# The first layer's experts moved from per-sequence masking to gathered slots, in a two-layer gated attention and expert kernel

## The reference

```python
x = x + tanh(g_xattn[0]) * cross(ctx, layernorm(x))      # u = 0: 16 heads, masked keys from ctx
x = x + tanh(g_ffn[0])   * ffn0(layernorm(x))            # u = 1
x = x + tanh(g_xattn[1]) * joint(layernorm(x), ctx)      # u = 2: keys of ctx and of x
x = x + tanh(g_ffn[1])   * ffn1(layernorm(x))            # u = 3: causal, then gated experts

def ffn0(x):                                             # the block that is changed
    attn_out = attention(x @ W_qkv + b_qkv)              # 16 heads of 16
    gate = softmax(x @ W_gate + b_gate)                  # 8 experts
    top_g, top_i = top_k(gate, 2)
    combine = sum(one_hot(top_i) * top_g)                # not normalised again
    expert_out = einsum('bsd,edf->bsef', x, W_experts) + b_experts
    return attn_out + einsum('bsef,bse->bsf', expert_out, combine)
```

## Time and profile before

| | us |
|---|---|
| median of 3 runs | 2615.38 |
| lowest and highest | 2613.62, 2620.35 |
| profiled execution, its own time | 2617.61 |
| its span, first to last instruction | 2615.9 |
| mean granted TensorE clock | 0.937 of full |
| PE busy in the span | 2282.1 (87%) |
| DVE busy | 1686.8 (64%) |
| ACT busy | 1362.3 (52%) |
| POOL busy | 978.5 (37%) |

### The profile page before, as it was taken

One profiled execution on the slowest core, in us unless ns is written; L12 is line 12 of the kernel. 1 busy time (PEld: TensorE's weight loads), 2 busy tenths in 40 slices (PEclk: granted clock), 3 DMA queues, 4 the chain that ended last, 5 costly groups with the idle time before them and its releaser, 6 DMA issues. The chain is left out here.

```text
span 2615.9 us, 52259 instructions
## 1 busy us (share of the span) xinstructions
PE 2282.1 (87%) x17492; PEld 1575.9 (60%) x17493; DVE 1686.8 (64%) x4481; ACT 1362.3 (52%) x2398; POOL 978.5 (37%) x1850
## 2 busy tenths in 40 slices
PE   2889999899999999999999999899848999999910
PEld 1445555555455556666666666666538999999910
DVE  4878886676767666777767668767563444443458
ACT  3889863454336346777777777767601222222211
POOL 5555412213122225333322247878602333333321
PEclk7999998999899999999999999999958999999965
DMA  7878623315134245544455445555180111111144
GB/s 216 206 192 208 148 67 82 88 38 122 30 88 95 65 99 135 116 116 113 112 118 120 107 116 109 122 133 129 42 277 27 34 36 37 36 36 32 35 173 156
DMA packets 209839, 275.49 MB, mean 105 GB/s; under 512 B 32606, under 2 KB 156489, under 8 KB 203370
## 3 DMA queue, kind: packets, MB, share of 16 engines
q1 hardware_dynamic: 196074, 242.38, 37.3%
q0 software_dynamic: 6912, 17.97, 2.2%
q10 hardware_dynamic: 6656, 12.58, 1.3%
HBM read 193.12 MB, written 80.64 MB: 105 GB/s over the span
## 5 line engine op out<-in xcount | busy, mean ns | idle before, releaser
L1035 ACT ACTIVATE ex<-t_ps 128x512 f32<-128x512 f32 (+1 forms) x1280 | 685.7, 579 | 203.0 <-PE t_ps L941 157.9
L1183 DVE TENSOR_REDUCE mx<-s_ps 128x2 f32<-128x512 f32 (+1 forms) x1024 | 659.9, 683 | 197.2 <-PE s_ps L912 125.2
L941 PE MATMUL t_ps<-qs,ks 123*128 123x256 bf16 x2048 | 355.5, 277 | 8.7 <-ACT ex L1035 3.7
L964 PE MATMUL pv_ps<-ex,va 128*17 128x256 f32 (+1 forms) x5120 | 318.1, 374 | 1.3 <-POOL ex L1087 1.3
L1029 ACT ACTIVATE qs<-tr_ps 27x2048 bf16<-27x2048 bf16 x128 | 239.2, 1869 | 108.3 <-PE tr_ps L925 105.5
L882 PE MATMUL pre_ps<-wexp,xt 128*128 128x512 f32 x512 | 270.5, 634 | 3.1 <-DVE moe L1242 2.2
L941 PEld LDWEIGHTS t_ps<-qs,ks 123*128 123x128 bf16 x2048 | 176.9, 98 | 156.1 <-ACT ex L1035 68.2
L1582 PEld LDWEIGHTS x_up_ps<-x_rows_t,x_wnow 128*128 128x128 f32 x2272 | 266.4, 193 | 5.3 <-issue 0.9
L1582 PE MATMUL x_up_ps<-x_rows_t,x_wnow 128*128 128x128 f32 x2272 | 267.0, 276 | 1.1 <-DVE x_pre L1645 0.7
L1592 PE MATMUL x_y_ps<-wdn,x_act 128*128 x1136 | 257.1, 379 | 0.7 <-DVE x_y L1653 0.7
L1612 ACT ACTIVATE x_rows_t<-x_rt_ps 128x256 f32<-128x256 f32 x72 | 27.6, 383 | 436.7 <-PE x_rt_ps L1571 436.7
(11 more groups left out here) (248 smaller groups left out, 3739.7 us busy)
## 6 DMA issues: line engine op xcount, KB each, us to landing
q_parts<-pq SPq DMA_DIRECT2D x128, 192.0 KB
qs<-q_parts SPq DMA_DIRECT2D x64, 384.0 KB, 4.9
qs<-q_parts SPq DMA_DIRECT2D x192, 128.0 KB, 5.8
k_parts<-pk SPq DMA_DIRECT2D x96, 192.0 KB
ks<-k_parts SPq DMA_DIRECT2D x96, 192.0 KB
ks<-k_parts SPq DMA_DIRECT2D x288, 64.0 KB
ks<-ctx_k_parts SPq DMA_DIRECT2D x64, 192.0 KB
ks<-ctx_k_parts SPq DMA_DIRECT2D x192, 64.0 KB
```

The lines of the kernel that those rows point to most:

```text
L941: last = pe.matmul(dst[:, t * T:(t + 1) * T], key[0:ROWS, h, t * P:(t + 1) * P], qs[q_at][0:ROWS, h, :], start=True, stop=True)
L964: last = pe.matmul(pv_ps[i * VS:i * VS + VW, q0:T], val[:, t, k * QH + i, :], e, start=r == 0 and t == 0, stop=r == srcs - 1 and t == NT - ...
L1035: act.activation(ex[:, n % EXPS, 0:w], t_ps[n % 2][:, 0:w], ACT.Exp).then_inc(t_read, 1)
L1183: dve.tensor_reduce(dst, s_ps[n % S_BANKS][:, :].rearrange("p (a b) -> p a b", a=dst.shape[-1]), AX.X, ALU.max).then_inc(s_read, 1)
```

## The change

The first layer's experts are run by slots as the second layer's are.

- **Cross jobs** (u = 0) get a tail after FIN: HNS, HNP and HNX normalise the updated x into `o`, STOREN writes it to memory, HT turns it (PE, ACT) and HG computes the gate logits of all tokens (PE, DVE).
- **Self jobs** no longer normalise x; LOADN brings the stored rows. GATE, GEXP, TOP, CT, MBIAS and EXPERT are gone, and FIN no longer adds the experts' share.
- **A chain for all tokens at once** begins when all sixteen HG are done: 23 RC steps on DVE with RX (ACT), RANK (PE), and sixteen RH, TH, NAME triples that find the row that each of 71 x 128 slots holds.
- **71 tiles** stand among self jobs 2 to 7 in the schedule's order (`tile_job`), 12 a job: XR gathers 128 rows (POOL, indirect DMA), XTT turns them (PE, ACT), XE multiplies by one expert's matrix, picked by a register loaded on PE and on DVE, and adds its bias (DVE), XS scatters the rows (POOL, indirect DMA).
- **Joint jobs** get LOADY and MOE: each token's two rows come back and are added to x with their weights by four DVE operations. LOADY of the first two jobs waits for all scatters.
- The second layer's `w1` and `wo` now share memory with the first layer's experts and are loaded at the first causal job's LOADX.

```diff
@@ STAGES, tile_job
+    "STOREN": [("sp", 0.5), ("wire", 6.0)], "LOADN": [("sp", 0.5), ("wire", 5.0)], "LOADY": [("sp", 0.5), ("wire", 6.5)], "MOE": [("dve", 1.95)],
+    "RC": [("dve", 0.95)], "RX": [("act", 0.42)], "RANK": [("pe", 0.9), ("dve", 0.72)],
+    "RH": [("dve", 0.67)], "TH": [("dve", 0.45), ("pool", 0.8)], "NAME": [("pe", 0.9), ("dve", 0.25)],
+    "XR": [("pool", 1.1), ("wire", 3.0)], "XTT": [("pe", 0.22), ("act", 0.39)], "XE": [("pe", 0.87), ("dve", 0.45)], "XS": [("pool", 1.1), ("wire", 3.5)],
+HOTS = 4
+CHUNKS = TOPK * TILES // HOTS
+NER, NY = 4, 3
+CHAIN = 23
+def tile_job(n):
+    return 1, 2 + n // 12
@@ job_steps
+    if u == 1:
+        s = add("LOADN", 0, ("STOREN", 0, b, 0), past("XT", 2))
+    else:
+        if u == 2:
+            y = add("LOADY", 0, *([("MOE", u, b - 2, 0)] if b >= 2 else [("XS", *tile_job(n), n) for n in range(SLOT_TILES)]))
+            x = add("MOE", 0, x, y)
...
-    if u == 1:
-        chain = add("GEXP", 0, add("GATE", 0, turned, ("FIN", u, b - 2, 0) if b >= 2 else None))
-        for n in range(TOPS):
-            chain = add("TOP", n, chain)
-        chain = add("MBIAS", 0, add("CT", 0, chain))
-        experts = [add("EXPERT", (t, e), chain) for t in range(NT) for e in range(0, E, 2)]
...
+    if u in (0, 3):
+        s = add("HNX", 0, add("HNP", 0, add("HNS", 0, s, ("HNX", u, b - 2, 0) if b >= 2 else None)))
+        if u == 0:
+            add("STOREN", 0, s)
+            s = add("HT", 0, s, past("HG", NQ))
@@ expert_steps
+    for n in range(SLOT_TILES):
+        add(of("XR", n), rc(CHAIN - 1), of("XTT", n - NER))
+        add(of("XTT", n), of("XR", n), of("XE", n - 2))
+        add(of("XE", n), of("XTT", n), of("XS", n - NY))
+        add(of("XS", n), of("XE", n))
@@ PE
-                    elif name == "EXPERT":
-                        t, e = k
-                        end_pre(step, pe.matmul(bank[:, :], xt_now[:, turn, t * P:(t + 1) * P], wexp[:, turn, e:e + 2, :].rearrange("p e n -> p (e n)"),
-                                                start=turn == 0, stop=ends), ends)
+                    elif name == "XTT":
+                        pe.wait_ge(er_loaded[k % NER], 16 * (k // NER + 1))
+                        for c in range(DC):
+                            last = pe.transpose(bank[:, c * P:(c + 1) * P], er[k % NER][:, c * P:(c + 1) * P], ident[:, :])
                         end_pre(step, last)
+                    elif name == "XE":
+                        wait_copied(pe, ("XTT", u, b, k))
+                        x = pe.value_load(expert_of[0:1, k:k + 1], min_val=0, max_val=E - 1)
+                        for c in range(DC):
+                            last = pe.matmul(bank[:, 0:D], ert[k % 2][:, c, :], wexp[:, c, bass.ds(x, 1), :].rearrange("p e n -> p (e n)"),
+                                             start=c == 0, stop=c == DC - 1)
+                        end_pre(step, last)
@@ POOL
+                    elif name == "XR":
+                        if k >= NER:
+                            wait_turned(pool, ("XTT", *tile_job(k - NER), k - NER))
+                        pool.indirect_dma_start(er[k % NER], None, n1_d.rearrange("b p t n -> (b p t) n"),
+                                                bass.IndirectOffsetOnAxis(ap=row_of[:, k:k + 1].bitcast(U32), axis=0)).then_inc(er_loaded[k % NER], 16)
+                    elif name == "XS":
+                        wait_copied(pool, ("XE", u, b, k))
+                        pool.indirect_dma_start(y1_d.rearrange("b p t n -> (b p t) n"), bass.IndirectOffsetOnAxis(ap=dest_of[:, k:k + 1], axis=0),
+                                                ey[k % NY], None, bounds_check=ROWS_OUT - 1, oob_is_err=False).then_inc(y_stored[k % NY], 16)
@@ DVE
+                    elif name == "XE":
+                        x = dve.value_load(expert_of[0:1, k:k + 1], min_val=0, max_val=E - 1)
+                        end_pre(step, dve.tensor_tensor(ey[k % NY], bank[:, 0:D], bexp[:, bass.ds(x, 1), :].rearrange("p e n -> p (e n)"), ALU.add))
+                    elif name == "MOE":
+                        for m in range(TOPK):
+                            for t in range(NT):
+                                last = dve.scalar_tensor_tensor(out=xs[x_at][:, t, :], in0=yb[b % 2][:, t * TOPK + m, :], scalar=first_share[:, b * NT + t, m:m + 1],
+                                                                in1=xs[x_at][:, t, :], op0=ALU.mult, op1=ALU.add)
```

More of the change, by code:

```diff
@@ L210, in job_steps @@
     if u < 2:
-        add("FIN", 0, *outs, *(experts if u == 1 else []))
+        s = add("FIN", 0, *outs)
     else:
@@ L227, in orders @@
         needs.update(job_steps(*job))
+    needs.update(expert_steps())
     ops = [(s, n) for s in needs for n in range(len(stages_of(s)))]
@@ L327, in rank @@
 def rank(op):
-    return 0 if op[0][0] in ("OT", "FIN", "M", "MT") else 1
+    return 0 if op[0][0] in ("OT", "FIN", "M", "MT", "RC", "RX", "RANK", "RH", "TH", "NAME") else 1
 ORDER, BEGUN, DONE = orders()
@@ L363 @@
 XN_AT = counted(of_kind("dve", "LNX"))
-LG_AT = counted(of_kind("dve", "GATE"))
-EXP_AT = counted(of_kind("act", "GEXP"))
-TOP_AT = counted(s for s in of_kind("dve", "TOP") if s[3] == TOPS - 1)
+RH_AT = counted(of_kind("dve", "RH"))
+TH_AT = counted(of_kind("dve", "TH"))
+MOE_AT = counted(of_kind("dve", "MOE"))
+NAMED_AT = counted(of_kind("pool", "TH"))
 def uses_before(kind, job, src=0):
@@ L393, in wait_stored, with rows_stored @@
     eng.wait_ge(stored[JOB[job] % NX], 16 * (JOB[job] // NX + 1))
+def rows_stored(b):
+    at = JOB[(0, b)] % NO
+    return sum(JOBS[j][0] == 0 for j in range(at, JOB[(0, b)] + 1, NO)), at
 class Chain:
@@ new lines, in attention_phase @@
+        tile_at = ring("tile_at", TOPK, [P, TILES]); row_at = ring("row_at", TOPK, [P, TILES])
+        ones = sb("ones", [P, P]); before_me = sb("before_me", [P, P])
+        tile_f = sb("tile_f", [P, COLS]); lane_f = sb("lane_f", [P, P]); name_f = ring("name_f", TOPK, [P, TILES])
+        expert_of = sb("first_expert_of", [P, COLS], I32); row_of = sb("first_row_of", [P, COLS], I32); dest_of = sb("first_dest_of", [P, COLS], U32)
+        work = sb("work", [P, (NER + 2 + NY) * D])
+        er = [work[:, k * D:(k + 1) * D] for k in range(NER)]
@@ L538, in attention_phase @@
+        named, dest, row_i = (ctx[1][:, :, :].rearrange("p t n -> p (t n)")[:, 3 * TILES * E + k * COLS:3 * TILES * E + (k + 1) * COLS] for k in range(3))
         lens = sb("lens", [B, 1], I32); lenf = sb("lenf", [B, 1])
@@ L1109, in _, with then @@
                 s = Chain(dve, dve_step, SETUP_STEPS)
-                wide = lambda z: z[:, :].unsqueeze(2).broadcast_to([P, NT, E])
-                at_of = {}
+                wide = lambda z: z[:, :].unsqueeze(2).broadcast_to([P, TILES, E])
+                tall = lambda z: z.unsqueeze(1).broadcast_to([P, TILES, E])
+                chain = 0
+                counts, ranks = ranked[:, 1, :, :], ranked[:, 0, :, :]
+                moved = None
+                def then(ins):
+                    s.done(ins)
+                    s.wait()
@@ L1118, in _ @@
                     j = JOB[(u, b)]
-                    r = b % 2 if u == 1 and name not in ("LNS", "LNX") else j % 2
+                    r = j % 2
                     nth_x, x_at = uses_before("x", (u, b))
```

399 lines of the change are left out of this document (278 added, 121 removed), and 1 row of the table STAGES.

## The result

The changed kernel takes 2625.03 us (median of 20 runs, 2617.7 to 2636.2), the kernel before 2618.53 beside it (20 runs): a ratio of 1.0028, 95% interval 1.0018 to 1.0039. The prediction was 2495 with 0.08 on slower. The profiled execution has a span of 2621.7.

What follows compares the result with a forecast made beforehand. PE alone was taken to bound the self stage (94% busy), with four resources near full in the cross stage. Self -162, cross +26, joint +8, seam +5 made -123 us, so 2617.6 became 2495; 2460 to 2530 at 0.55, range 2420 to 2585.

Steps and rivals of the forecast that it cites:

- PE's work is 573 (94% of 612) - 316 + 143 = 400 us: Self stage: PE's present work, less 316 us of removed groups, plus 143 us for tiles, naming and register loads.
- The price of a tile: Self stage, PE: two transposes and two float32 matmuls, 1.41 us a tile, 100 us for 71 tiles.
- the seam: Start of the joint stage: LOADY's wait for the last scatter and queued stacking DMAs cost 5 us, 0 to 20.
- the 0.89 that was assumed: Self stage after the change: PE busy share, making 400 us of work a 450 us stage, a gain of 162.
- POOL's time: Self stage: 313 to 422 us of POOL work with 142 indirect DMAs; POOL 75 to 90% busy.
- the slower rival: Self stage: indirect DMAs waiting in POOL's list before M delay it and starve PE; kernel 2685 us; chance 0.09.
- hidden when matmuls are queued ahead: Self stage: PE's register load, bare otherwise, costs 0 to 0.77 us a tile; 0.35 taken, 25 us in all.
- DVE's busy time: Self stage: 416 - 237 + 126 = 305 us of DVE work, including 55 us of register loads.
- MOE at 8 us: Joint stage: 39 us of DVE operations cost 0.5 us a job, 8 us, of 0 to 39; 50 by POOL contention.
- during which PE works on these jobs: Cross-stage tail: some 75 dependent ranking operations take 50 to 80 us while PE works on two to four self jobs.
- the cross stage: Normalising, storing, turning and gate logits added to each cross job cost 1.6 x 16 = 26 us, between 11 and 40.
- the rivals: Whole kernel: POOL bound or late tiles 0.16, everything hides 0.13, cross stage pays more 0.07, slower 0.09.

Runs made afterwards that it cites:

- k7: k4 with 62 of the 71 tiles left out and joint jobs adding stored normalised rows instead of expert rows: 0.9416 of the kernel before.
- after: The changed kernel itself, with no further edit: 2625.03 us, 1.0028 of the kernel before.
- t1: k4 with only the 71 gathers as plain transfers of 128 rows, scatters still indirect: 0.9767 of the kernel before.
- t3: k4 unchanged, run again on another chip beside t1: 0.9989 of the kernel before.
- r1: The changed kernel unchanged, run again on another chip: 2642.6 us, 1.0115 of the kernel before.
- r2: k4 unchanged, run again on the chip of r1: 2616.4 us, 0.9999 of the kernel before.
- s1: k4 unchanged, run once more on the chip of r2: 1.0003 of the kernel before.
- s2: k2 unchanged, run again on the chip of s1: 0.9964 of the kernel before.
- k3: The changed kernel with three of MOE's four DVE operations left out in each joint job: 0.9899 of the kernel before.
- k4: The changed kernel, complete, with each tile's register loads on PE and DVE issued one tile ahead: 2568.34 us, 0.9824 of the kernel before.
- k1: The changed kernel without PE's register load per tile (tile n takes expert n modulo 8), DVE's load kept: 0.9892 of the kernel before.
- k2: k1 with DVE's register load left out as well: 2566.1 us, 0.9812 of the kernel before.
- r3: k6 unchanged, run again on the chip of r2: 0.9977 of the kernel before.
- k6: k4 with MOE as four schedule steps of one operation each, on another chip: 1.0002 of the kernel before.
- k8: k4 with MOE in four steps and the ranking chain ranked three jobs later: 2595.7 us, 0.9915 of the kernel before.
- r4_costs: k8 with the schedule's list of durations corrected to measured ones, run beside r2: 0.9854 of the kernel before.
- s3: k4 with both gather and scatter of each tile as plain transfers of 128 rows: 0.9748 of the kernel before.

## Why the prediction was wrong

**The first step that failed: "PE's work is 573 (94% of 612) - 316 + 143 = 400 us".** The changed kernel's PE works 473 us in its self stage. k7, with nine tiles, gives the base by itself (394 for the start of the stage in after, 399 in k7; the fences are after and k7):

```profile
394.00:972.00 578.00, 473.35 (x3330) 309.24 (x3331) 316.58 (x676) 305.96 (x572) 316.69 (x453) 0.92 0.53 135
```

```profile
399.00:808.00 409.00, 362.72 (x2956) 240.57 (x2957) 297.14 (x616) 280.66 (x509) 191.33 (x326) 0.95 0.62 154
```

From 362.7 go nine tiles (13) and names (19.8 with RANK, forecast 18): 330 us for sixteen self jobs without experts. The forecast had 573 - 316 = 257. The trace of before gives the same without any run: in its self stage PE is busy for 578 us, and for 336 if the records of the four removed groups are left out. They took 242 us with them, not 316. The price of a tile was right: 448.4 in t1 less 362.7 is 86 us for 62 tiles, 1.38 each, forecast 1.41. What was taken out was priced too high. 27 of the 512 expert records, and a like share of the others, lie before the stage begins. And matmuls of neighbouring groups overlap in the records, so the busy times of groups add up to more than PE's busy time. In the kernel before, fifteen groups of the self stage sum to 682 us beside a busy PE of 578 (window, then the two largest groups):

```profile
362.00:979.00 617.00, 578.25 (x3333) 318.66 (x3331) 424.21 (x1040) 280.97 (x512) 143.94 (x282) 0.95 0.31 76
```

```profile
L882 PE MATMUL pre_ps<-wexp,xt 128*128 128x512 f32 x485 | 256.9, 636 | 3.1 <-DVE moe L1242 2.2 <-DVE va L1167 0.8
L941 PE MATMUL t_ps<-qs,ks 123*128 123x256 bf16 x510 | 88.1, 280 | 3.4 <-ACT qs L1029 2.2 <-ACT ex L1035 0.9
```

Removing 316 us of group time removes less of the engine's. Another 15 us were moved in: the first joint jobs' keys and values are now computed in the self stage (64 records of w1x in place of 16, 17.5 us for 4.3, and 14 for 8, 3.7 for 2.2; after's group below). It fits with this that the seam came out 22 us shorter instead of 5 longer.

```profile
L940 PE MATMUL pre_ps<-xt,w1x 128*128 128x256 f32 x64 | 17.5, 398 | 0.0
```

At the 0.89 that was assumed, those 73 us make 82 of stage. And 0.89 was right once the stops were gone: t1 has 448.4 in 509, 88%.

**The second: "an indirect DMA stands in POOL's list" as a cost on POOL alone.** POOL's time came out at the low end (312 us in 568, forecast 313 to 422), 55% of the stage and not 75 to 90%. POOL did stand before the scatters, 81 us for DVE's additions, as the slower rival has it. What series of two kinds of indirect transfers do to the other engines, 61 us on the chip of t3, no row of before shows. The rows of indirect transfers are from a stage where they stand singly, and there PE is hardly ever idle (before):

```profile
1990.00:2500.00 510.00, 504.72 (x3470) 474.82 (x3469) 202.05 (x347) 109.15 (x207) 173.83 (x280) 1.00 0.11 34
```

**The third: "hidden when matmuls are queued ahead", 25 us for PE's register load, nothing bare on DVE.** Moving both ahead gave 26 us on one chip (r1, r2), and leaving them out 11 more (s1, s2). On k4's chip the two loads cost 53 us of the self stage (k3, k4), 17 of it DVE's (k1, k2). PE's load lay within its 0 to 55 us, but it was written into PE's work and lies in the tile's chain; DVE's was counted as work only. That DVE's busy time came out near the forecast (308 us for 305) is luck: the forecast holds 55 us of register loads, which aren't in the busy time.

Together: 450 + 82 + 61, with the 28 us (25 / 0.89) counted for the load taken out and some 12 put in for what it costs in the stage (591 to 577 from r1 to r2, 578 to 570 from after to t3), is 577; found 578. The parts come from different chips, so it is a balance, no proof. With k4's chip it divides otherwise: 450 + 82 - 28 + 53 for the loads is 557, and k3's self stage of 573 leaves 16 for stops. PE is busy for 450 us in k4's self stage and for 448 in t1's, so the 82 us stand on both chips; how the rest falls to loads and to indirect transfers differs.

**The fourth: MOE at 8 us**, of 0 to 39. The joint closings spread by 34 us more (557.7 for 523.5), and k3 and r3 give 27 to 30 of it back. PE was the bound, but MOE as one block delays the maxima for which PE's banks wait: r3 gives back 30 us of the stage while DVE still spends 41 us on the operations.

MOE's own time was 50.8 us on DVE, 64 operations of 0.79 us, where the forecast had 39, and 50 by the contention that it named. That contention shows plainly (durations in ns, least, median and most, of MOE in the changed kernel and in r3; then POOL beside the block at 1177.65):

```profile
L1400 DVE SCALAR_TENSOR_TENSOR xs<-work,first_share,xs x64: 472/581/1423, 838.2 to 1335.9; 128x256 f32<-128x256 f32 x64
```

```profile
L1408 DVE SCALAR_TENSOR_TENSOR xs<-work,first_share,xs x64: 468/478/1433, 821.7 to 1301.0; 128x256 f32<-128x256 f32 x64
```

```profile
1178.04 1.22 POOL L1229 TENSOR_TENSOR pk<-ak,pk 128x512 bf16<-128x512 f32 x1
1179.22 1.34 POOL L1225 TENSOR_TENSOR aq<-aq,pq 128x512 f32<-128x512 f32 x1
```

The 21 operations with no POOL instruction beside them took 0.47 to 0.49 us each. Of the 43 with one, 29 took 0.82 to 1.42. In r3 only 24 of 64 fall beside one, and their sum is 41.0 us. The Trainium skill (SBUF — State Buffer, "Who interferes with whom") says that a DVE instruction with two SBUF inputs contends with a GpSimd instruction that reads SBUF. The trace agrees. What the stage grew by, 34 us, is less than DVE's 50.8, since DVE was not full there.

**"during which PE works on these jobs".** The ranking chain's 14.6 us at a standstill, with the half clock behind them, were costed at nothing. k6 and k8, one chip and one edit apart, price them at 21 us of the whole, 15 of it in the self stage, though k8's tiles start 16 us later. The balance above has no term of its own for it, since t1, whose 88% it uses, has the same block.

**What held:** the cross stage (33 for 26, within 11 to 40; which part of it makes the difference was not tried), cross jobs 19.7 us, 284 records of tile matmuls (0.30 us busy each for 0.25). ACT's wait for MT fell from 84.7 us to 44.8. Self jobs are 36 us (577.5 / 16), not 27 to 29. Of the rivals none came true. The slower one had its sign but not its place: by ACT's wait, M was not late.

**A version that beats both:** k4_hoist on the chip with few stops (0.982); r4_costs on a chip with more (0.985, r2 beside it 1.000). r4 has not been run on the first chip.

## What to carry to other kernels

The busy time of a PE group is not what goes away with it. Check the sum of an engine's groups against its busy time in that stretch before subtracting, take only what lies inside the stretch, and ask what moves into the room. Give an inner chain's small steps (a register load, a block of DVE operations) their bare time until a trace hides them, put loads one tile ahead, and write measured durations into a schedule. Compare variants on the same chip only: here one kernel gave 0.982 of the kernel before on one chip and 0.999 to 1.000 on two others, while the kernel before itself differed by 0.2%. (The first chip was used in one group of runs only, so chip and group aren't separated there; chip 5, used in two, gave 2616.4 and 2618.6.)

## What the hardware showed that was not expected

- With gathers and scatters both indirect, in series on POOL with gaps of 0.3 us, PE, DVE and ACT stop together, in r2 for up to 3.7 us, mostly behind two or more transfers of a series; with either kind plain one or two short stops are left. On three chips these are 15 us and more in the kernels with the loads moved, on the fourth 9. Why they come, and why one chip has fewer, stays open.
- An addition on DVE with both inputs in SBUF, 128 x 256 in float32, takes 0.48 us alone and up to 1.4 beside a POOL instruction (MOE, above).
- POOL spends 1.0 us on an indirect transfer of 128 rows of 1 KB and 0.55 us on a plain one (s3, 71 of each kind, two records missing; first the scatter):

```profile
L1204 POOL DMA_DIRECT2D first_expert_rows<-work x71 | 39.4, 556 | 83.2 <-DVE work L1397 80.1 <-issue 2.9
L1200 POOL DMA_DIRECT2D work<-normed x69 | 37.4, 545 | 7.0 <-PE pre_ps L1003 6.9
```

- The granted clock is 0.92 over the self stage of the changed kernel and 0.95 over that of before, though PE does less: it now has more short idle times, and several are followed by half clock, as in r2 at 542 us.
